# A fused attention and FFN block in f32: transposing y itself, and scaling F by 1/std instead of y

## The chip, the cores and the metric

One core of one Trainium2 chip runs the whole program. The metric is the device time of one execution in microseconds, the median of several runs. TensorE (PE) multiplies matrices and transposes, VectorE (DVE) and ScalarE (ACT) work on its results, GpSimd (POOL) computes small powers, SyncE (SP) issues nearly all DMAs. The engines run on their own and meet only through semaphores.

## The reference

The input x is 8 x 1024 x 256 in f32. What is computed is:

```python
x = x + _layernorm(_L0_attn_ref(_layernorm(x), Wq, Wk, Wv, Wo))   # causal, scaled by 1/16
x = x + _layernorm(_L0_ffn_ref(_layernorm(x), W, b, logits, u))

def _layernorm(x, axis=-1, eps=1e-05):
    m = jnp.mean(x, axis=axis, keepdims=True)
    v = jnp.var(x, axis=axis, keepdims=True)
    return (x - m) / jnp.sqrt(v + eps)

def _L0_ffn_ref(x, W, b, logits, u):
    gumbel = -jnp.log(-jnp.log(u))
    idx = jnp.argmax(jax.nn.log_softmax(logits) + gumbel)
    return jnp.einsum('btd,de->bte', x, W[idx]) + b[idx]
```

The attention has one head of 256 columns; one of eight 256 x 256 FFN matrices is chosen by idx. There are no scales and shifts in the norms.

## The kernel before, in words

The kernel takes the 8 batches one after the other: the first written out, six in a loop on each engine, the last written out with an order of its own. A batch has 1024 rows, 8 tiles of 128; most steps work on a tile or on a pair of tiles.

Each engine runs through a written order of steps, such as PE_ORDER, ACT_ORDER, DVE_ORDER and POOL_ORDER (lines 66 to 73), the PE_LAST and other orders for the last batch, and the PE_BEFORE and other orders for what comes ahead of the first batch. A letter is a kind of step and a number its tile or pair: S scores, M mask and row maximum (DVE), E exponential (ACT), T transposes of the probabilities, V the values, O probabilities times values, R the residual y = x + norm(O) (DVE), N statistics of y, K the normalised yn (ACT), Y the transposes of yn, F the FFN product, U its variance, Z the output, and for the next batch L statistics of x, H its normalising, X its transposes and G the product that the scores need. C is the variance of O.

A product in nearly full precision is made of three f32r passes (`product`, line 800): each operand is split into a rounded half, *_hi, which ACT writes from PSUM, and the rest, *_lo, which DVE writes as PSUM minus *_hi (`subtract_lo`, line 610; its rows have line 613). The lower half's end frees the PSUM bank. Four banks are passed round among the jobs T, V, O, Y, F, X, G in the order in which PE meets them. A job waits (`take_bank`, line 790) until the job four before it has been drained, and until its inputs have been. The scores have four banks of their own (the tensor score), two for even and two for odd tiles.

Around y: R (L741) writes y. N (lines 744 to 757) takes mean and variance of a pair, and writes minus the mean (y_nm) and variance + eps (y_ve). POOL's N step raises y_ve to -0.5 (y_rstd, L387) and makes y_shift = y_nm * y_rstd (L393). ACT's K step (L583) makes yn = y * y_rstd + y_shift, tile by tile. PE's Y step (L932) transposes yn in four pieces, ACT and DVE split it into yT_hi and yT_lo, and PE's F step multiplies with the split weights wf_hi and wf_lo. DVE's F step (L762) adds the bias, one operation for a pair; ACT squares and sums f_sb (L591), DVE's U makes f_ve (L769), POOL f_rstd, and Z (L778) is f_sb * f_rstd + y. For the last batch, Y, F, U, Z have five units, the last two of one tile each, and PE fills gaps with passes on zeros (D, keep_warm).

The FFN matrix and the bias are centred over the output columns ahead of the loop, so that the mean of F is zero: ACT's sums of rows (L470), DVE's neg_mean (L646), ACT's centred (L474). Then ACT makes wf_hi (L502) and DVE wf_lo (L661), both also ahead of the loop, and PE waits for them before the first F. The products of W matrices at L865 are plain f32 matmuls of 256 columns.

## Time and profile before

| | |
|---|---|
| Median of 3 runs | 425.5 us (425.34 to 428.11) |
| Span of the profiled execution | 424.3 us |
| Around the span, against the median | 1.2 us |
| PE busy | 414.0 us, 98% |
| DVE busy | 339.8 us, 80% |
| ACT busy | 299.1 us, 71% |
| POOL busy | 118.3 us, 28% |
| Chain that ended last | PE 93%, DMA 2%, ACT 2%, DVE 1% |
| Granted PE clock | 1.0 in the first slice, 0.9 or more in all others |

The profiled execution has no separate time; its span is what the rows are measured in. A matmul's end is modelled, so the durations of neighbouring matmuls overlap, and distances from start to start are the better measure. On DVE and ACT, too, an operation's start follows its forerunner's start by less than the duration that is shown. Where equal operations follow each other, a timeline merges them to one row with a count (x2).

### The profile page before, as it was taken

What the parts mean: (1) busy time and instruction counts of PE and PEld (TensorE: products, weight loads), DVE (VectorE), ACT (ScalarE), POOL (GpSimd) and SP (SyncE); (2) the same over time, 40 slices, a digit from 0 to 9 for tenths busy, and PEclk for the clock granted to TensorE, in tenths of its full rate; (3) what the DMA queues carried; (4) which work ended last, traced back from release to release, by engine and by line L of the source; (5) the groups of instructions that cost most, each with busy time, mean ns of one, the idle gap of its engine ahead of it and who ended that gap; (6) DMA issues with size and microseconds to landing.
All of it is one profiled execution on the core that took longest, in us unless ns stands there. A gap on an engine that the chain in (4) does not pass through costs nothing.

```text
span 424.3 us, 9812 instructions
## 1 busy us (share of the span) xinstructions
PE 414.0 (98%) x3045; PEld 393.2 (93%) x3045; DVE 339.8 (80%) x1010; ACT 299.1 (71%) x854; POOL 118.3 (28%) x237
## 2 busy tenths in 40 slices
PE   7999999999999999999999999999999999999993
PEld 7789999999999999999999999999999999999993
DVE  4578778987898878887788878898788887876776
ACT  5886877668766687568866687666885678756563
POOL 3103333232322232123421323223232224302133
PEclk9999999999999999999999999999999999999998
DMA  6310012110120101201021001201012000020003
GB/s 198 90 49 26 26 25 76 52 39 14 51 81 18 49 25 42 82 9 40 25 66 57 25 25 48 76 25 49 13 37 99 0 0 0 25 75 2 2 0 101
DMA packets 18951, 18.46 MB, mean 44 GB/s; under 512 B 1140, under 2 KB 18932, under 8 KB 18932
## 3 DMA queue, kind: packets, MB, share of 16 engines
q1 hardware_dynamic: 18660, 17.96, 13.5%
q10 hardware_dynamic: 272, 0.26, 0.2%
q8 instruction: 10, 0.16, 0.2%
q14 instruction: 9, 0.07, 0.1%
HBM read 9.83 MB, written 8.39 MB: 43 GB/s over the span
## 4 chain that ended last, share of the span: by engine, by line
PE 93%; DMA 2%; ACT 2%; DVE 1%; issue 0%; POOL 0%; SPq 0%; POOLq 0%; DVEq 0%
PE bank L805 54%; PE score L805 23%; PE bank L908 7%; PE bank L932 3%; PE bank L819 3%; DMA wq<-in_L_attn_Wq_dram 1%; DMA bias_raw<-in_L_ffn_b_dram 1%; PE score L891 1%; PE score L847 0%; PE bank L865 0%; POOL f_rstd L387 0%; PE score L835 0%; DVE out_sb L778 0%; ACT squares_junk L591 0%; ACT sums_junk L470 0%
## 5 line engine op out<-in xcount | busy, mean ns | idle before, releaser
L387 POOL TENSOR_TENSOR o_rstd<-o_ve,minus_half 128x1 f32<-128x1 f32 x64 | 35.2, 550 | 193.8 <-DVE o_ve L735 193.8
L805 PE MATMUL bank<-v_hi,pT_lo 128*128 128x256 f32 x288 | 84.6, 294 | 0.0
L805 PE MATMUL bank<-v_hi,pT_hi 128*128 128x256 f32 x288 | 81.4, 283 | 0.0
L805 PE MATMUL bank<-v_lo,pT_hi 128*128 128x256 f32 x288 | 81.3, 282 | 0.0
L805 PE MATMUL score<-xT_hi,g_lo 128*128 128x384 f32 (+4 forms) x176 | 63.7, 362 | 0.0
L805 PE MATMUL score<-xT_hi,g_hi 128*128 128x384 f32 (+4 forms) x176 | 61.1, 347 | 0.0
L805 PE MATMUL score<-xT_lo,g_hi 128*128 128x384 f32 (+4 forms) x176 | 61.1, 347 | 0.0
L549 ACT ACTIVATE probs<-neg_scores,neg_max 128x128 f32<-128x128 f32 (+3 forms) x64 | 49.7, 776 | 14.0 <-DVE neg_max L707 13.5
L805 PEld LDWEIGHTS bank<-v_lo,pT_hi 128*128 128x128 f32 x288 | 55.0, 191 | 0.4
L805 PEld LDWEIGHTS bank<-v_hi,pT_lo 128*128 128x128 f32 x288 | 54.9, 191 | 0.3
L805 PEld LDWEIGHTS bank<-v_hi,pT_hi 128*128 128x128 f32 x288 | 54.9, 191 | 0.0
L707 DVE CUSTOM_DVE_ANT_0 neg_scores<-score,mask 128x128 f32<-128x128 f32 (+3 forms) x64 | 48.2, 755 | 7.6 <-PE score L805 7.5
L574 ACT ACTIVATE squares_junk<-bank 128x256 bf16<-128x256 f32 x64 | 24.5, 383 | 40.3 <-PE bank L805 39.8
L613 DVE TENSOR_TENSOR pT_lo<-bank,pT_hi 128x384 fp32r<-128x384 f32 (+2 forms) x96 | 49.6, 551 | 0.8
L441 ACT ACTIVATE pT_hi<-bank 128x384 fp32r<-128x384 f32 (+2 forms) x96 | 43.1, 484 | 2.2 <-PE bank L908 2.0
L908 PE MATMUL bank<-ident,probs 128*128 128x128 f32 x288 | 42.0, 273 | 0.0
L741 DVE SCALAR_TENSOR_TENSOR y<-bank,o_rstd,x_sb 128x256 f32<-128x256 f32 x64 | 30.8, 481 | 11.1 <-POOL o_rstd L387 11.0
L591 ACT ACTIVATE squares_junk<-f_sb 128x256 bf16<-128x256 f32 x64 | 26.3, 419 | 16.7 <-DVE f_sb L762 16.7
L583 ACT ACTIVATE yn<-y,y_shift,y_rstd 128x256 f32<-128x256 f32 x64 | 35.0, 597 | 4.3 <-POOL y_shift L393 4.3
L387 POOL TENSOR_TENSOR f_rstd<-f_ve,minus_half 128x2 f32<-128x2 f32 (+1 forms) x33 | 24.1, 731 | 49.6 <-DVE f_ve L769 49.6
L805 PE MATMUL bank<-wf_hi,yT_lo 128*128 128x256 f32 x128 | 37.3, 292 | 0.4 <-DVE yT_lo L613 0.4
L805 PE MATMUL bank<-wvo_hi,xT_lo 128*128 128x256 f32 x128 | 36.9, 288 | 0.0
(112 smaller groups left out, 1130.5 us busy)
## 6 DMA issues: line engine op xcount, KB each, us to landing
x_sb<-in_L_attn_x_dram SPq DMA_DIRECT2D x32, 256.0 KB, 2.7
out_dram<-out_sb SPq DMA_DIRECT2D x31, 256.0 KB, 2.1
wq<-in_L_attn_Wq_dram ACTq DMA_DIRECT2D x1, 256.0 KB, 4.1
wk<-in_L_attn_Wk_dram SPq DMA_DIRECT2D x1, 256.0 KB, 4.4
wv<-in_L_attn_Wv_dram SPq DMA_DIRECT2D x1, 256.0 KB, 4.2
wo_raw<-in_L_attn_Wo_dram SPq DMA_DIRECT2D x1, 256.0 KB, 4.5
wf_raw<-in_L_ffn_W_dram SPq DMA_DIRECT2D x1, 256.0 KB, 2.7
out_dram<-out_sb SPq DMA_DIRECT2D x2, 128.0 KB, 2.1
```

Source lines behind the costliest of these rows:

```text
L387: return nc.gpsimd.tensor_tensor(dst[:, n0:n1], ve[:, n0:n1], minus_half[:, n0:n1], ALU.pow)
L441: nc.scalar.activation(dst, src, ACT.Identity).then_inc(hi_ready, 1)
L549: nc.scalar.activation(probs[:, n % 2, here], neg_scores[:, n % 2, here], ACT.Exp, scale=-1.0, bias=neg_max[:, n:n + 1], accum_out=exp_sum ...
L574: nc.scalar.activation(squares_junk[:, 0, n, :], cols(job.bank, D), ACT.Square, accum_out=o_ss[:, n:n + 1])
L583: last = nc.scalar.activation(yn[:, p, t % 2, :], y[:, t, :], ACT.Identity, bias=y_shift[:, t:t + 1], scale=y_rstd[:, t:t + 1])
L591: last = nc.scalar.activation(squares_junk[:, 1, t, :], f_sb[:, p, t % 2, :], ACT.Square, accum_out=f_ss[:, t:t + 1])
L613: nc.vector.tensor_tensor(dst, src, hi.bitcast(f32), ALU.subtract).then_inc(bank_drained[job.bank], 1)
L707: nc.vector.tensor_tensor_reduce(out=masked.rearrange("p (h w) -> p h w", h=h), in0=score[:, n % 2, 0:h, 0:w], in1=mask[:, here].rearrange ...
L741: nc.vector.scalar_tensor_tensor(out=y[:, n, :], in0=cols(job.bank, D), scalar=o_rstd[:, n:n + 1], in1=x_tile(b, n), op0=ALU.mult, op1=ALU ...
L805: last = nc.tensor.matmul(dst, l, r, start=(i == 0), stop=(i == len(passes) - 1))
L819: last = nc.tensor.transpose(cols(job.bank)[:, (2 * k + t) * PART:(2 * k + t + 1) * PART], xn[:, 2 * p + t, k * PART:(k + 1) * PART], iden ...
L908: last = nc.tensor.transpose(cols(job.bank)[:, (t - t0) * PART:(t - t0 + 1) * PART], probs[:, n % 2, t * PART:(t + 1) * PART], ident[:, :])
```

## The change

The mean of y is no longer taken away before the FFN. Instead the FFN matrix, already centred over its columns, is centred over its rows of input too, so that a constant in y contributes nothing. PE computes the means itself: two f32 products of a 128 x 128 matrix that is full of 1/256 with the two halves of wf, into score's bank for odd tiles, before S2 of the first batch. DVE subtracts them from wf after M2 of the first batch. ACT's wf_hi follows E3 and DVE's wf_lo follows M5 of the first batch; both have left the orders ahead of the loop.

PE's Y step transposes y, and waits for the drained O jobs of its tiles instead of for yn. ACT's K steps are gone, and so are y_nm, y_shift and yn. POOL's N step makes y_rstd alone. DVE's F step waits for y_rstd as well, and is one operation for each tile: bank * y_rstd + bias, 128 x 256.

The diff, without the declarations of buffers and semaphores:

```diff
@@ -65,8 +65,8 @@
 
     PE_ORDER = """S0 V0 S1 V1 T0 S2 T1 S3 O0 V2 T2 O1 S4 T3 V3 O2 S5 O3 T4 S6 T5 S7 X0 Y0 O4 T6 O5 T7 O6 X1 Y1
         O7 F0 G0 Y2 X2 F1 X3 F2 Y3 G1 G2 F3 G3"""
-    ACT_ORDER = """V0 E0 E1 V1 T0 E2 O0 T1 V2 T2 O1 E3 H0 T3 V3 E4 O2 O3 E5 T4 K0 T5 E6 K1 X0 Y0 O4 T6 E7 O5 T7
-        H1 H2 O6 Y1 H3 X1 O7 K2 G0 Y2 F0 X2 K3 X3 F1 Y3 F2 G1 G2 F3 G3"""
+    ACT_ORDER = """V0 E0 E1 V1 T0 E2 O0 T1 V2 T2 O1 E3 H0 T3 V3 E4 O2 O3 E5 T4 T5 E6 X0 Y0 O4 T6 E7 O5 T7
+        H1 H2 O6 Y1 H3 X1 O7 G0 Y2 F0 X2 X3 F1 Y3 F2 G1 G2 F3 G3"""
     DVE_ORDER = """M0 M1 L0 V0 M2 T0 V1 L1 T1 C0 M3 R0 V2 L2 T2 M4 C1 V3 T3 R1 N0 M5 C2 C3 R2 R3 N1 M6 T4 T5 M7
         X0 Y0 C4 R4 T6 C5 L3 R5 T7 C6 N2 R6 X1 Y1 C7 F0 R7 N3 G0 Y2 F1 U0 X2 Z0 X3 F2 U1 Y3 U2 Z1 G1
         F3 Z2 U3 G2 G3 Z3"""
@@ -75,8 +75,8 @@
 
     PE_LAST = """V0 S0 V1 S1 T0 S2 V2 T1 S3 O0 T2 O1 S4 T3 S5 O2 T4 O3 S6 V3 T5 O4 S7 Y0 T6 O5 T7 O6 Y1 F0 O7
         Y2 F1 F2 Y3 D11 Y4 F3 D12 F4"""
-    ACT_LAST = """E0 V0 V1 T0 E1 V2 T1 E2 O0 E3 T2 O1 T3 E4 T4 O2 O3 E5 K0 E6 V3 T5 O4 Y0 T6 E7 O5 K1 T7 O6 Y1
-        K2 F0 O7 Y2 K3 Y3 F1 K4 Y4 F2 F3 F4"""
+    ACT_LAST = """E0 V0 V1 T0 E1 V2 T1 E2 O0 E3 T2 O1 T3 E4 T4 O2 O3 E5 E6 V3 T5 O4 Y0 T6 E7 O5 T7 O6 Y1
+        F0 O7 Y2 Y3 F1 Y4 F2 F3 F4"""
     DVE_LAST = """M0 V0 M1 M2 V1 T0 V2 T1 C0 M3 M4 C1 R0 T2 R1 T3 N0 M5 C2 R2 C3 T4 M6 R3 V3 N1 C4 T5 R4 M7 Y0
         T6 C5 R5 T7 N2 C6 F0 R6 Y1 U0 N3 C7 Y2 F1 R7 N4 F2 Y3 U1 Z0 Z1 Y4 U2 F3 U3 F4 Z2 U4 Z3 Z4"""
     POOL_LAST = """C0 C1 C2 N0 C3 N1 C4 C5 N2 C6 U0 N3 C7 N4 U1 U2 U3 U4"""
@@ -85,8 +85,8 @@
 
 
     PE_BEFORE = "D22 W0 W1 D13 X0 A0 X1 D25 W2 G0 D6 X2 X3 G1 A1 G2 G3"
-    ACT_BEFORE = "W0 H0 J0 H1 X0 A0 X1 B0 H2 H3 G0 J1 X2 X3 G1 U0 A1 U1 G2 U2 G3 E0"
-    DVE_BEFORE = "L0 L1 W1 B0 J0 L2 L3 X0 A0 X1 W2 B1 G0 X2 X3 U0 G1 A1 U1 G2 G3"
+    ACT_BEFORE = "W0 H0 J0 H1 X0 A0 X1 B0 H2 H3 G0 J1 X2 X3 G1 U0 A1 U1 G2 G3 E0"
+    DVE_BEFORE = "L0 L1 W1 B0 J0 L2 L3 X0 A0 X1 W2 B1 G0 X2 X3 U0 G1 A1 G2 G3"
 
     def steps_of(text):
         return [(w[0], int(w[1:])) for w in text.split()]
...
@@ -377,6 +376,7 @@
             pool.wait_ge(memsets, 1)
             nc.gpsimd.affine_select(out=ident[:, :], in_=ident[:, :], compare_op=ALU.not_equal, fill=1.0, base=0,
                                     pattern=[[-1, PART]], channel_multiplier=1).then_inc(consts_ready, 1)
+            nc.gpsimd.memset(averaging[:, :], 1.0 / D)
             nc.gpsimd.memset(mask[:, :], 0.0).then_inc(memsets, 1)
             pool.wait_ge(memsets, 2)
 
@@ -410,7 +410,7 @@
                     elif kind == "N":
 
                         pool.wait_ge(y_ve_ready, b * NP + n + 1)
-                        scales(y_nm, y_ve, y_rstd, y_shift, t0, t1).then_inc(y_shift_ready, 1)
+                        rstd(y_rstd, y_ve, t0, t1).then_inc(y_rstd_ready, 1)
                     elif kind == "U":
 
                         pool.wait_ge(f_ve_ready, b * NP + n + 1)
@@ -498,7 +498,7 @@
                         centred(2 + m, wf_raw[:, m, :], wf[:, m, :])
                     centred(4, bias_raw[:, :], bias[:, :]).then_inc(wf_centred, 1)
                 else:
-                    act.wait_ge(wf_centred, 1)
+                    act.wait_ge(wf_twice_centred, 1)
                     nc.scalar.activation(wf_hi[:, :, :], wf[:, :, :], ACT.Identity).then_inc(wf_hi_ready, 1)
 
             for kind, n in steps_of(ACT_BEFORE):
@@ -534,7 +534,7 @@
                     nc.scalar.activation((wvo_hi if n else a_hi)[:, :, :],
                                          cols(job.bank).rearrange("p (m n) -> p m n", m=KC), ACT.Identity, scale=1.0 if n else -SCALE).then_inc(hi_ready, 1)
 
-            def sequence(b, last_one=False):
+            def sequence(b, last_one=False, first=False):
                 def at(kind, n, g=0):
                     return Job(b, last_one, kind, n, g)
 
@@ -549,6 +549,8 @@
                         nc.scalar.activation(probs[:, n % 2, here], neg_scores[:, n % 2, here], ACT.Exp, scale=-1.0,
                                              bias=neg_max[:, n:n + 1],
                                              accum_out=exp_sums[:, n:n + 1]).then_inc(probs_ready, 1)
+                        if first and n == 3:
+                            ffn_weights(2)
                     elif kind == "T":
                         for g, (t0, t1) in enumerate(t_groups(n)):
                             job = at("T", n, g)
@@ -576,13 +578,6 @@
 
                         nc.scalar.activation(o_ez[:, n:n + 1], exp_sums[:, n:n + 1], ACT.Square,
                                              scale=EPS ** 0.5).then_inc(o_squares, 1)
-                    elif kind == "K":
-
-                        act.wait_ge(y_shift_ready, b * NP + n + 1)
-                        for t in range(t0, t1):
-                            last = nc.scalar.activation(yn[:, p, t % 2, :], y[:, t, :], ACT.Identity,
-                                                        bias=y_shift[:, t:t + 1], scale=y_rstd[:, t:t + 1])
-                        last.then_inc(yn_ready, 1)
                     elif kind == "F":
                         job = at("F", n)
 
@@ -592,7 +587,7 @@
                                                         accum_out=f_ss[:, t:t + 1])
                         last.then_inc(f_squares, 1)
 
-            sequence(0)
+            sequence(0, first=True)
             with act.Fori(1, B - 1) as b:
                 sequence(b)
             sequence(B - 1, True)
@@ -655,11 +650,6 @@
                     negative_means(0, 2, 1)
                 elif kind == "U" and n == 0:
                     negative_means(2, 5, 2)
-                elif kind == "U":
-
-                    dve.wait_ge(wf_hi_ready, 1)
-                    nc.vector.tensor_tensor(wf_lo[:, :, :], wf[:, :, :], wf_hi[:, :, :].bitcast(f32),
-                                            ALU.subtract).then_inc(wf_ready, 1)
                 elif kind == "B" and n == 0:
                     dve.wait_ge(choice_loaded, 32)
                     nc.vector.tensor_reduce(lse[:, 0:1], logits[:, :], AX.X, ALU.max, negate=True).then_inc(choice_dve, 1)
@@ -688,7 +678,7 @@
 
             dve.wait_ge(mask_ready, 1)
 
-            def sequence(b, last_one=False):
+            def sequence(b, last_one=False, first=False):
                 def at(kind, n, g=0):
                     return Job(b, last_one, kind, n, g)
 
@@ -709,6 +699,17 @@
                                                        in1=mask[:, here].rearrange("p (h w) -> p h w", h=h),
                                                        scale=1.0, scalar=3e38, op0=ALU.add, op1=ALU.min,
                                                        accum_out=neg_max[:, n:n + 1]).then_inc(max_ready, 1)
+                        if first and n == 2:
+
+                            dve.wait_ge(wf_means_ready, 1)
+                            nc.vector.tensor_tensor(wf[:, :, :], wf[:, :, :],
+                                                    score[:, 1:2, 1, 0:D].broadcast_to([PART, KC, D]),
+                                                    ALU.subtract).then_inc(wf_twice_centred, 1)
+                        elif first and n == 5:
+
+                            dve.wait_ge(wf_hi_ready, 1)
+                            nc.vector.tensor_tensor(wf_lo[:, :, :], wf[:, :, :], wf_hi[:, :, :].bitcast(f32),
+                                                    ALU.subtract).then_inc(wf_ready, 1)
                     elif kind == "T":
                         for g, (t0, t1) in enumerate(t_groups(n)):
                             job, here = at("T", n, g), slice(t0 * PART, t1 * PART)
@@ -752,17 +753,19 @@
                             last = nc.vector.bn_aggr(y_mv[:, t, :], y_stats[:, t, :])
                         last.then_inc(y_mv_ready, 1)
                         dve.wait_ge(y_mv_ready, b * NP + n + 1)
-                        nc.vector.tensor_scalar(y_nm[:, t0:t1], y_mv[:, t0:t1, 0], -1.0, None, ALU.mult)
                         nc.vector.tensor_scalar(y_ve[:, t0:t1], y_mv[:, t0:t1, 1], EPS, None,
                                                 ALU.add).then_inc(y_ve_ready, 1)
                     elif kind == "F":
                         job = at("F", n)
 
                         dve.wait_ge(bank_full[job.bank], job.used + 1)
-                        nc.vector.tensor_tensor(f_sb[:, p, here, :],
-                                                cols(job.bank, (t1 - t0) * D).rearrange("p (t d) -> p t d", t=t1 - t0),
-                                                bias[:, None, :].broadcast_to([PART, t1 - t0, D]),
-                                                ALU.add).then_inc(bank_drained[job.bank], 1)
+                        dve.wait_ge(y_rstd_ready, b * NP + n + 1)
+                        for t in range(t0, t1):
+                            last = nc.vector.scalar_tensor_tensor(out=f_sb[:, p, t % 2, :],
+                                                                  in0=bank[job.bank][:, (t - t0) * D:(t - t0 + 1) * D],
+                                                                  scalar=y_rstd[:, t:t + 1], in1=bias[:, :],
+                                                                  op0=ALU.mult, op1=ALU.add)
+                        last.then_inc(bank_drained[job.bank], 1)
                     elif kind == "U":
 
                         dve.wait_ge(f_squares, b * NP + n + 1)
...
@@ -884,6 +887,15 @@
 
                             g = g_job(b, 2 * (n // (NT // 2)) + 1)
                             pe.wait_ge(bank_drained[g.bank], g.used + 1)
+                        if first and n == 2:
+
+                            pe.wait_ge(wf_centred, 1)
+                            for k in range(KC):
+                                means = nc.tensor.matmul(score[:, 1, 1, 0:D], averaging[:, :], wf[:, k, :], start=(k == 0),
+                                                         stop=(k == KC - 1))
+                            means.then_inc(wf_means_ready, 1)
+                        elif first and n == 5:
+                            pe.wait_ge(wf_twice_centred, 1)
                         h, w = pieces(n)
                         if w < 2 * PART:
 
@@ -925,12 +937,11 @@
                                 ).then_inc(bank_full[job.bank], 1)
                     elif kind == "Y":
 
-                        pe.wait_ge(yn_ready, b * NP + n + 1)
                         job = at("Y", n)
-                        take_bank(job)
+                        take_bank(job, *(at("O", t) for t in range(t0, t1)))
                         for i, (k, t) in enumerate((k, t) for k in range(KC) for t in range(t0, t1)):
                             last = nc.tensor.transpose(cols(job.bank)[:, i * PART:(i + 1) * PART],
-                                                       yn[:, p, t % 2, k * PART:(k + 1) * PART], ident[:, :])
+                                                       y[:, t, k * PART:(k + 1) * PART], ident[:, :])
                         last.then_inc(bank_full[job.bank], 1)
                     elif kind == "F":
                         if first and n == 0:
```

## Rows read from the trace of the kernel before

**Rows 1.** page, part 1: busy us, share of the span, instructions of each engine.
```profile
PE 414.0 (98%) x3045; PEld 393.2 (93%) x3045; DVE 339.8 (80%) x1010; ACT 299.1 (71%) x854; POOL 118.3 (28%) x237
```

**Rows 2.** waits of TensorE: engine, what, releaser: us in total, times, longest.
```profile
PE score L835 <- POOL ident L378: 1.7, 1, 1.7
PE bank L932 <- ACT yn L583: 1.1, 1, 1.1
PE score L847 <- DMA wq<-in_L_attn_Wq_dram: 0.7, 1, 0.7
PE score L891 <- DVE wvo_lo L682: 0.6, 1, 0.6
PE bank L805 <- DVE xT_lo L613: 0.4, 1, 0.4
PE bank L805 <- DVE yT_lo L613: 0.4, 2, 0.3
```

**Rows 3.** groups by line and shape: busy us, mean ns, idle before, releaser.
```profile
L583 ACT ACTIVATE yn<-y,y_shift,y_rstd 128x256 f32<-128x256 f32 x64 | 35.0, 597 | 4.3 <-POOL y_shift L393 4.3
...
L741 DVE SCALAR_TENSOR_TENSOR y<-bank,o_rstd,x_sb 128x256 f32<-128x256 f32 x64 | 30.8, 481 | 11.1 <-POOL o_rstd L387 11.0
L778 DVE SCALAR_TENSOR_TENSOR out_sb<-f_sb,f_rstd,y 128x256 f32<-128x256 f32 x64 | 28.1, 480 | 2.7 <-POOL f_rstd L387 2.7
...
L762 DVE TENSOR_TENSOR f_sb<-bank,bias 128x512 f32<-128x512 f32 x31 | 21.4, 689 | 7.6 <-PE bank L805 7.6
...
L755 DVE TENSOR_SCALAR y_nm<-y_mv 128x2 f32<-128x2 f32 x31 | 5.3, 170 | 1.1
...
L707 DVE CUSTOM_DVE_ANT_0 neg_scores<-score,mask 128x384 f32<-128x384 f32 x8 | 4.5, 558 | 2.3 <-PE score L805 2.3
...
L865 PE MATMUL bank<-wo,wT 128*128 128x256 f32 x8 | 1.9, 379 | 0.0
...
L762 DVE TENSOR_TENSOR f_sb<-bank,bias 128x256 f32<-128x256 f32 x2 | 0.8, 422 | 0.0
```

**Rows 4.** VectorE in order of time, third batch: start us, us, what, idle before.
```profile
165.57 0.69 DVE L762 TENSOR_TENSOR f_sb<-bank,bias 128x512 f32<-128x512 f32 x1 [0.16 <-PE bank L805]
166.18 0.16 DVE L769 TENSOR_SCALAR f_ve<-f_ss 128x2 f32<-128x2 f32 x1
166.25 0.68 DVE L613 TENSOR_TENSOR xT_lo<-bank,xT_hi 128x512 fp32r<-128x512 f32 x1
167.21 0.88 DVE L778 SCALAR_TENSOR_TENSOR out_sb<-f_sb,f_rstd,y 128x256 f32<-128x256 f32 x2 [0.28 <-POOL f_rstd L387]
168.01 0.69 DVE L613 TENSOR_TENSOR xT_lo<-bank,xT_hi 128x512 fp32r<-128x512 f32 x1
```

**Rows 5.** TensorE in order of time, same batch: the transposes of Y3.
```profile
167.23 0.60 PE L932 MATMUL bank<-ident,yn 128*128 128x128 f32 x4
```

**Rows 6.** VectorE in order of time, first batch: v_lo of pair 1.
```profile
29.73 0.68 DVE L613 TENSOR_TENSOR v_lo<-bank,v_hi 128x512 fp32r<-128x512 f32 x1
```

**Rows 7.** TensorE in order of time, first batch: first matmul of V2.
```profile
30.70 0.28 PE L805 MATMUL bank<-wvo_hi,xT_lo 128*128 128x256 f32 x1
```

**Rows 8.** TensorE in order of time, the end: Y4 and F4.
```profile
416.09 0.44 PE L932 MATMUL bank<-ident,yn 128*128 128x128 f32 x2 [1.14 <-ACT yn L583]
...
418.18 0.36 PE L805 MATMUL bank<-wf_hi,yT_lo 128*128 128x256 f32 x1 [0.25 <-DVE yT_lo L613]
```

**Rows 9.** VectorE in order of time, the end: out_sb of pair 1, yT_lo of Y4.
```profile
416.81 0.88 DVE L778 SCALAR_TENSOR_TENSOR out_sb<-f_sb,f_rstd,y 128x256 f32<-128x256 f32 x2 [0.27 <-POOL f_rstd L387]
417.61 0.42 DVE L613 TENSOR_TENSOR yT_lo<-bank,yT_hi 128x256 fp32r<-128x256 f32 x1
```

**Rows 10.** busy us of PE, PEld, DVE, ACT, POOL by stretch; clock, DMA share, GB/s.
```profile
415.00:420.00 5.00, 2.78 (x26) 2.39 (x26) 3.88 (x13) 3.11 (x14) 2.33 (x5) 1.00 0.27 86
420.00:425.00 5.00, 0.00 (x0) 0.00 (x0) 1.31 (x4) 0.13 (x2) 0.72 (x1) 0.69 0.38 128
```

More of the change, by code:

```diff
@@ L188, in sandwich_block_kernel @@
         y = sb("y", [PART, NT, D])
-        yn = sb("yn", [PART, NP, 2, D])
         yT_hi = sb("yT_hi", [PART, NP, KC, 2, PART], f32r)
@@ L210, in sandwich_block_kernel @@
         y_ve = sb("y_ve", [PART, NT])
-        y_nm = sb("y_nm", [PART, NT])
-        y_shift = sb("y_shift", [PART, NT])
         y_rstd = sb("y_rstd", [PART, NT])
@@ L238, in sandwich_block_kernel @@
         ident = sb("ident", [PART, PART])
+        averaging = sb("averaging", [PART, PART])
         mask = sb("mask", [PART, S])
@@ L267, in sandwich_block_kernel @@
         y_ve_ready = sem("y_ve_ready")
-        y_shift_ready = sem("y_shift_ready")
-        yn_ready = sem("yn_ready")
+        y_rstd_ready = sem("y_rstd_ready")
         f_squares = sem("f_squares")
@@ L297, in sandwich_block_kernel @@
         wf_centred = sem("wf_centred")
+        wf_means_ready = sem("wf_means_ready")
+        wf_twice_centred = sem("wf_twice_centred")
         wf_hi_ready = sem("wf_hi_ready")
@@ L781, in sequence @@
                         last.then_inc(out_ready, 1)
-            sequence(0)
+            sequence(0, first=True)
             with dve.Fori(1, B - 1) as b:
```

## The prediction

> **What bounds the kernel now.** I read the busy times first. TensorE is busy 414.0 of 424.3 us, VectorE 339.8, ScalarE 299.1 [rows 1]; the reader is to see that only 10.3 us of the span are left in which TensorE does nothing at all. The view of waits comes second: TensorE waits 1.7 + 1.1 + 0.7 + 0.6 + 0.4 + 0.4 = 4.9 us in the whole run, six entries, none of which is met once per batch [rows 2]. So in the batches TensorE never stands still, and the work that the change takes away (ScalarE's normalising of y, VectorE's negated mean) isn't on the path. What can move the time is (a) work added to TensorE, (b) waits that arise because VectorE hands something over later than today, and (c) the two ends of the run. The profiled execution has a span of 424.3 us; the median of the three runs is 425.5, 1.2 above it. I work against the span and add 1.2.
>
> **Removed.** ScalarE loses the 64 yn operations, 35.0 us [rows 3]. Their cover: TensorE waited for yn once, 1.1 us [rows 2], so for the batches this is worth nothing. VectorE loses y_nm, 31 operations; between two short ones it takes some 0.08 us of the queue, so about 0.3 us per batch. GpSimd loses the y_shift product and its drain; nobody waits on GpSimd for it but ScalarE's yn. PE's Y step has the same four transposes, and waits for y instead of yn; y exists earlier than yn, always. It keeps its place in TensorE's order, so nothing behind it moves.
>
> **Added in each batch: F.** Today F is one addition of 128x512 at 689 ns; afterwards it is two 128x256 multiply-and-adds, of the kind of L741 (481 ns, PSUM and SBUF in) or L778 (480) [rows 3]. Counted from start to start, today's F takes 166.18 - 165.57 = 0.61 us of the queue, and a pair of L778 takes 168.01 - 167.21 = 0.80 [rows 4]. Each F thus makes VectorE 0.20 us later, four times a batch, 0.8 us, against 0.3 given back. VectorE has idle time for that on average (85 us over the run), but what counts is the place. Behind F of the second pair stand f_ve and then xT_lo of pair 2, at 166.25, which ends at 166.93 [rows 4]. That step frees the bank that TensorE's Y3 takes at 167.23 [rows 5]: a margin of 0.30 us. What is the least distance from a VectorE end to TensorE's start? The last F of the run did wait: yT_lo ended at 417.61 + 0.42 = 418.03 and TensorE began at 418.18 [rows 8, 9], 0.15 us. Later by 0.20, the margin is 0.10 and TensorE stands still for 0.05 us. (F1 itself is paced by TensorE, [rows 4] show it idle for 0.16 before, so lateness from F0 isn't added.) Seven batches have this order: **+0.35 us**. F also waits for a second semaphore, y_rstd, which is long there; if the second wait instruction costs some 0.05 us behind the first, the stall is 0.1 per batch, +0.7 in all. Its lower bound is nothing, if the margin is a little larger than I read; the upper bound is that all four F's lateness arrives, below. I take 0.35, since the two rows give it directly.
>
> On whether such an F is dear, the row comes first: L778 has two f32 tensors from SBUF and takes 480 ns, L741 with one of them in PSUM takes 481 [rows 3]. The Trainium skill, page "Vector Engine (DVE) Microarchitecture Reference", list of pitfalls at its end, says that a scalar_tensor_tensor with two SBUF sources that are not bf16 runs at half throughput. By that, L778 would have to be dearer than L741 by another pass over 256 elements, and it isn't; F would then cost 0.53 us more, and the batches would be VectorE's. The trace disagrees, and I go by the row.
>
> **Added once: second centring of the FFN weights.** (1) TensorE gets two f32 (not f32r) products of 256 columns ahead of S2 of the first batch. Of that kind is L865: four calls make 8 instructions, 1.9 us busy [rows 3], so two calls make 4 instructions, 0.95 us by that, and TensorE has no free time there: **+0.9**. Bounds: 0.75, since the modelled ends overlap (379 ns is the mean of one, but 8 fill 1.9 us), and 1.0 with the change from one kind of matmul to the other. (2) VectorE subtracts the means, 128x512 like today's F, 0.6 us of its queue, between M2 and T0. M2 is a step before which VectorE waits for TensorE (2.3 us in eight, [rows 3]), so earlier VectorE time doesn't cover it. Behind it, v_lo of pair 1 at 29.73, ends 30.41 [rows 6], and frees the bank of TensorE's V2, which begins at 30.70 [rows 7]: margin 0.28. Later by 0.60 the wait is 0.60 - 0.28 + 0.15 = **+0.47**. Steps behind it are late by the same 0.6, but TensorE is by then 0.47 later itself. Bounds: 0, if the work that left the preamble makes up for it, and 0.6, the whole subtraction. (3) wf_hi and wf_lo move from ahead of the loop into the first batch, behind E3 and M5. wf_lo's 0.6 us lands where VectorE waits for ScalarE and GpSimd soon after; wf_hi's operation lands on a ScalarE that loses 2.2 us of yn soon after. Ahead of the loop VectorE no longer waits for wf_hi, but TensorE's wait there is for wvo_lo (0.6, [rows 2]), made before. Nothing either way. The memset of the averaging matrix is short and stands behind ident.
>
> **The end.** TensorE's 1.1 us wait for yn is before Y4, at 416.09 [rows 8]. Without it Y4 goes right after the filler. But its yT_lo stands in VectorE's queue behind the two out_sb of pair 1, which start at 416.81 and wait for a square sum and GpSimd, not for yn; yT_lo starts at 417.61 as they end [rows 9]. That chain begins with ScalarE's squares of F1, which follow Y3. So what is late next is f_rstd, and the 1.1 us come back as TensorE idling later. The single-tile F3 and F4 are in that chain and go from 422 to 481 ns each [rows 3]: **+0.1**.
>
> **Sum:** 0.9 + 0.47 + 0.35 + 0.1 = +1.8, with a share of the second wait +1.9: span 426.2, time 427.4 us, 0.4% above the median.
>
> **Rivals.**
> A, VectorE in the way (slower). Lateness of F isn't absorbed at TensorE's places, since all four F steps, two-wait overhead included (0.26 each), less 0.3, reach the T1 of the next batch: 0.72 us a batch, 5.0 in seven, 424.3 + 5.0 + 1.4 + 0.1 + 1.2 = 432.0. It decides once VectorE has no idle between F3 and M2 of the next batch. Against it: that idle before M2, 2.3/8 = 0.29 us each [rows 3]. For it: only 0.15 to 0.3 us of margin at several places.
> B, nothing stalls. VectorE and ScalarE start the first batch earlier since the wf work left the preamble, and F's 0.2 us is absorbed: only 0.9 of TensorE work, time 426.4.
> C, the wait for yn did set the end. Y4, F3 and their squares come 1.1 us earlier: 427.4 - 1.1 = 426.3. For it, the wait is real; against it, the place of yT_lo in VectorE's queue.
> D, faster: ScalarE's 35 us make TensorE run closer. Even if all 4.9 us of its waits [rows 2] went, 425.5 - 4.9 + 0.9 = 421.5. The start's 1.7 and 0.7 are for ident and Wq, which the change doesn't touch.
> E, the clock at the end. The granted clock is 1.00 in 415 to 420, with TensorE busy for 2.78 of 5 us, and 0.69 on average in the next 5, where it does nothing [rows 10], so it does fall to the 1.2 GHz level after a rest. With Y4 and F3 moved up, TensorE rests longer ahead of F4; if the clock fell there, F4's 0.7 us double: 428.1. The Trainium skill, "TensorE: Matmul & The Clock Gate", Part 1, says that the engine is slowed by rest and freed by activity; the trace agrees in this row, but the rest ahead of F4 would stay under 1.2 us.
>
> **How the numbers follow.** Forecast 0.51; B 0.20; C 0.13; A 0.08; D 0.03; E 0.03; the rest is unnamed. B and C lie within 1.1 us below the forecast, and both together would give 425.3, so the range begins at 425.4; it ends at 429.3, where not quite half of A's lateness arrives. About 1% (4.3 us) is what a measurement of this kernel can tell from no change. Slower by more needs A almost in full or more than one mishap: 0.08. Faster by more needs D: 0.03. Within: 0.89.
>
> **What would show it.** Right: TensorE busy rises by about 0.9 us, with 4 new instructions around 28 us; ScalarE falls by some 35 us; f_sb rows of 480 ns x64; a new TensorE wait for v_lo of about 0.3 to 0.5 us once; a wait for xT_lo of 0.05 us in each batch, so a period of TensorE from batch to batch that is up by under 0.1. The yn wait is gone, and before F4 TensorE waits over 1 us for yT_lo. Wrong: a period up by 0.5 us or more (A), an unchanged period and no v_lo wait (B), or a last out_sb that comes 1 us earlier after F0 (C).

## The result, and the profile after

| | before | after |
|---|---|---|
| Median of the compared runs | 426.08 us (425.34 to 428.11, 14 runs) | 428.69 us (427.86 to 432.43, 14 runs) |
| Ratio after to before | | 1.0065, interval 1.0051 to 1.0080 |
| Span of the profiled execution | 424.3 us | 426.5 us |

The change makes the kernel 2.6 us slower, 0.65%, which is within the 1% that the prediction counts as no change, and inside its range. Forecast were 427.4 us in time and 426.2 in span.

The page after, busy times:

```profile
PE 416.5 (98%) x3049; PEld 394.7 (93%) x3049; DVE 343.6 (81%) x1009; ACT 268.2 (63%) x790; POOL 112.0 (26%) x205
```

ScalarE is busy 30.9 us less than in [rows 1], where some 35 was forecast, and none of it reached the time. TensorE has four instructions more and is busy for 2.5 us more. The forecast gave it 0.9, so most of the difference isn't new work. Its waits, in the columns of [rows 2]:

```profile
PE score L838 <- POOL ident L377: 1.7, 1, 1.7
PE bank L808 <- DVE yT_lo L608: 1.4, 2, 0.7
PE bank L808 <- DVE xT_lo L608: 0.7, 1, 0.7
PE score L850 <- DMA wq<-in_L_attn_Wq_dram: 0.6, 1, 0.6
PE score L903 <- DVE wvo_lo L672: 0.2, 1, 0.2
```

The sum is 4.6 us, 0.3 less than before. The wait for yn is gone, and the wait for yT_lo has gone from 0.4 to 1.4 in its place. F's group on VectorE has another form, and the averaging is a new one on TensorE (columns as in [rows 3]):

```profile
L764 DVE SCALAR_TENSOR_TENSOR f_sb<-bank,y_rstd,bias 128x256 f32<-128x256 f32 x64 | 28.0, 478 | 5.6 <-PE bank L808 5.2
...
L894 PE MATMUL score<-wf,averaging 128*128 128x256 f32 x4 | 1.0, 380 | 0.0
```

**Where the time went.** TensorE shows no rest in the loop, so its own marks divide the run: S0, the first scores of each batch. Its rows in the timeline of TensorE (start us, us) of the first, second and last batch, before:

```profile
23.34 0.71 PE L891 MATMUL score<-xT_first,g_first 128*128 128x128 f32 x4 [0.64 <-DVE wvo_lo L682]
...
73.45 0.61 PE L891 MATMUL score<-xT_first,g_first 128*128 128x128 f32 x4
...
374.36 0.61 PE L891 MATMUL score<-xT_first,g_first 128*128 128x128 f32 x4
```

and after:

```profile
22.49 0.71 PE L903 MATMUL score<-xT_first,g_first 128*128 128x128 f32 x4 [0.20 <-DVE wvo_lo L672]
...
73.94 0.60 PE L903 MATMUL score<-xT_first,g_first 128*128 128x128 f32 x4
...
376.31 0.61 PE L903 MATMUL score<-xT_first,g_first 128*128 128x128 f32 x4
```

| us | start of S0 | first batch | six batches | last part | span |
|---|---|---|---|---|---|
| before | 23.34 | 50.11 | 300.91 | 49.9 | 424.3 |
| after | 22.49 | 51.45 | 302.37 | 50.2 | 426.5 |
| difference | -0.85 | +1.34 | +1.46 | +0.3 | +2.2 |

The first batch costs 1.34 us, nearly all of it the averaging and the subtraction, as forecast. The six batches cost 0.24 us each, where the forecast had 0.05, and they have no new wait in the view of waits, which doesn't list the shortest ones. The start is no firm gain: over all seven traces of versions of the kernel before, S0 starts between 22.61 and 24.34 us (mean 23.5), over the seven of the kernel after between 22.49 and 23.26 (mean 22.9).

What makes six batches longer in which TensorE shows as busy all the time? Counting starts of its instructions in 124 to 174 us (columns as in [rows 10]), before and after:

```profile
124.00:174.00 50.00, 50.00 (x369) 47.73 (x369) 41.93 (x126) 36.08 (x104) 14.40 (x28) 1.00 0.14 42
```

```profile
124.00:174.00 50.00, 50.00 (x367) 47.67 (x366) 42.17 (x125) 32.05 (x96) 13.60 (x24) 1.00 0.13 41
```

At the same granted clock of 1.00 it starts two matmuls less in 50 us. Worked out from all rows of the timeline, the 256-column products of V stand 119.6 ns apart from start to start after and 116.9 before, those of F 119.7 and 117.7 (means within a step). A batch has 48 of each: 48 x 2.7 + 48 x 2.0 = 0.23 us. The work is the same, at a closer or wider spacing. This isn't the whole account: the 24 products of 512 columns of G stand about 2 ns closer after, which gives back 0.05 us, and a short stall of 0.09 us at F3 is new (below, under F on VectorE).

### The profile page after: what moved, and what is told of

Its sections match the earlier page's. It is cut to its first block, busy times and chain, and to the rows that moved or that the text cites. A ratio compares the mean times of both kernels' runs of the same rounds, so it can differ in the third digit from the quotient of the medians.

```text
span 426.5 us, 9687 instructions
## 1 busy us (share of the span) xinstructions
PE 416.5 (98%) x3049; PEld 394.7 (93%) x3049; DVE 343.6 (81%) x1009; ACT 268.2 (63%) x790; POOL 112.0 (26%) x205
## 4 chain that ended last, share of the span: by engine, by line
PE 92%; DVE 3%; issue 1%; ACT 1%; POOL 1%; DMA 1%; POOLq 0%; SPq 0%; DVEq 0%
PE bank L808 54%; PE score L808 23%; PE bank L920 7%; PE bank L943 3%; PE bank L822 3%; PE score L903 1%; DMA bias_raw<-in_L_ffn_b_dram 1%; DVE f_sb L764 1%; ACT sums_junk L470 0%; POOL f_rstd L387 0%; DVE xT_lo L608 0%; DVE out_sb L781 0%; ACT xn L464 0%; DVE x_stats L622 0%; POOL mask L380 0%
## 5 line engine op out<-in xcount | busy, mean ns | idle before, releaser
L808 PE MATMUL bank<-wf_hi,yT_hi 128*128 128x256 f32 x128 | 36.2, 283 | 0.0
```

The costliest lines, as they stand in the source:

```text
L808: last = nc.tensor.matmul(dst, l, r, start=(i == 0), stop=(i == len(passes) - 1))
```

## The experiments

Each ratio is to the kernel before, run beside the variant, and its interval follows in brackets.

The theory going in was that the first batch is slower by the new work, and the loop by where the buffers lie: the change takes out yn (8192 bytes of each partition), y_nm and y_shift (32 bytes each) and adds averaging (512), and everything declared behind them moves. Summed from the declarations, a, wvo and wf lie at 64 modulo 128 bytes before and at 0 after. The rivals: VectorE's longer F makes many short waits that the view doesn't list, or the batches differ by chance from one version or run to another.

**after_pad64**: 64 unused bytes put back ahead of the weights.

```diff
+        pad64 = sb("pad64", [PART, 16])
         wq = sb("wq", [PART, KC, D])
```

> The changed kernel with an unused buffer of 64 bytes a partition ahead of wq, so that wvo and wf again begin at 64 modulo 128 bytes, as they did in the kernel before; nothing else differs. The trace of the changed kernel has V and F matmuls of 256 columns 120 ns apart where they were 117 to 118 apart before, and a batch period of 50.15 us against 49.92. Theory A (address): the moving operand's place modulo 128 bytes sets the distance; V and F come back to 117 to 118 ns, the batch period to 49.95 to 50.00, the time falls by 1.0 to 1.4 us. Theory B (VectorE in the way, as predicted): the pad changes nothing; period 50.15, same time.

Measured: 428.71 us (426.96 to 431.06), ratio 1.0055 (1.0019 to 1.0090), span 425.8. S0 in its trace:

```profile
74.64 0.61 PE L904 MATMUL score<-xT_first,g_first 128*128 128x128 f32 x4
...
375.84 0.61 PE L904 MATMUL score<-xT_first,g_first 128*128 128x128 f32 x4
```

Six batches take 301.20 us instead of 302.37, the last part 0.2 less, the first 0.07 less: 1.4 us between S0 and the end come from nothing but the place of buffers. V's spacing is 117.2 ns and F's 117.3. The median of the times does not show this by itself, since its interval is as wide as the effect; the traces do, and before_again and after_again (below) say how far they can be trusted.

**before_pad64**: the same 64 bytes in the kernel before, the same edit.

> The kernel before with the same unused 64 bytes ahead of wq, which moves wvo and wf to 0 modulo 128 bytes, the place they have in the changed kernel. Theory A (address): V and F matmuls go from 117-118 to 120 ns apart, the batch period from 49.92 to 50.10, plus 1.2 to 1.5 us, though no instruction differs. Theory B (VectorE in the way): no change, period 49.92.

Measured: 427.20 us (425.94 to 428.10), ratio 1.0012 (0.9989 to 1.0035), span 424.3. First batch 50.23, six batches 301.42: 0.5 us more than before in six batches, not 1.2. V and F went to 119.0 and 118.8 ns, but the 512-column products of G from 233.4 to 232.4, faster. So the places of a, wvo and wf modulo 128 matter, but aren't the whole rule: the theory wanted 1.2 to 1.5 us.

**before_fpairs**: F as two additions of 128x256, without a scale.

```diff
-                        nc.vector.tensor_tensor(f_sb[:, p, here, :],
-                                                cols(job.bank, (t1 - t0) * D).rearrange("p (t d) -> p t d", t=t1 - t0),
-                                                bias[:, None, :].broadcast_to([PART, t1 - t0, D]),
-                                                ALU.add).then_inc(bank_drained[job.bank], 1)
+                        for t in range(t0, t1):
+                            last = nc.vector.tensor_tensor(f_sb[:, p, t % 2, :],
+                                                           bank[job.bank][:, (t - t0) * D:(t - t0 + 1) * D],
+                                                           bias[:, :], ALU.add)
+                        last.then_inc(bank_drained[job.bank], 1)
```

> The kernel before with F's addition of the bias made in two operations of 128x256 instead of one of 128x512; no scaling, no second wait. It isolates VectorE's lateness. Theory B as the prediction had it: each F takes 0.80 instead of 0.60 us of VectorE's queue, TensorE waits 0.05 us for xT_lo before Y3 in each batch, period 49.97, plus 0.3 to 0.5 us. Theory A gives no more than that here. If lateness of all four F reached TensorE, the period would be 50.6 and the time 5 us more.

Measured: 426.80 us, ratio 1.0004 (0.9980 to 1.0027), span 425.3, of which 1.0 is a later first S0 (24.31); first batch 50.12, six batches 300.91, the same as before.

**before_stt**: F as two multiply-and-adds with a constant in the place of y_rstd.

```diff
+                            last = nc.vector.scalar_tensor_tensor(out=f_sb[:, p, t % 2, :],
+                                                                  in0=bank[job.bank][:, (t - t0) * D:(t - t0 + 1) * D],
+                                                                  scalar=1.0, in1=bias[:, :],
+                                                                  op0=ALU.mult, op1=ALU.add)
```

> The kernel before with F made in two scalar_tensor_tensor of 128x256 (bank * 1.0 + bias), without the wait for y_rstd. before_fpairs used two additions, which took only 0.07 us more of the queue (margin ahead of Y3 0.23 instead of 0.30) and stopped nothing. Theory B (VectorE's lateness by 0.20 us per F): here the margin is 0.10, TensorE waits before Y3, the period goes from 49.92 to 49.96, +0.3 us in all, and if the changed kernel's remaining 0.045 us per batch (with 64 bytes of padding) came from the second wait, this one stays at 49.92.

Measured: 426.07 us, ratio 0.9989 (0.9964 to 1.0013), span 423.9, six batches 300.81. The groups of F in the two, before_fpairs first:

```profile
L763 DVE TENSOR_TENSOR f_sb<-bank,bias 128x256 f32<-128x256 f32 x64 | 24.1, 417 | 6.3 <-PE bank L806 4.9
```

```profile
L763 DVE SCALAR_TENSOR_TENSOR f_sb<-bank,bias 128x256 f32<-128x256 f32 x64 | 24.2, 419 | 6.2 <-PE bank L807 4.9
```

The multiplication costs nothing, 419 ns to 417. The change's F has 478: the 60 ns come with the scale read from memory, one value for each partition. And a pair in VectorE's order of time, before_stt and then after:

```profile
165.21 0.76 DVE L763 SCALAR_TENSOR_TENSOR f_sb<-bank,bias 128x256 f32<-128x256 f32 x2
165.89 0.16 DVE L771 TENSOR_SCALAR f_ve<-f_ss 128x2 f32<-128x2 f32 x1
```

```profile
166.47 0.88 DVE L764 SCALAR_TENSOR_TENSOR f_sb<-bank,y_rstd,bias 128x256 f32<-128x256 f32 x2
167.26 0.16 DVE L772 TENSOR_SCALAR f_ve<-f_ss 128x2 f32<-128x2 f32 x1
167.33 0.68 DVE L608 TENSOR_TENSOR xT_lo<-bank,xT_hi 128x512 fp32r<-128x512 f32 x1
```

0.68 us of the queue against 0.79, and 0.61 for the one addition of before [rows 4]: of the 0.18 us by which F is longer, 0.07 come from two operations in the place of one, and 0.11 from the scale. So neither before_fpairs nor before_stt makes VectorE as late as the change does, and that their batches are no longer doesn't show that the change's F is free.

**after_nomeans**: after_pad64 without the averaging products, without the subtraction, and with wf_hi waiting for the first centring only. It leaves the second centring out.

> The changed kernel with the 64 bytes of padding, and without the second centring: neither the two products with the averaging matrix nor the subtraction of the means are made, so the output lacks the removal of y's mean. Expected by the prediction's terms: the first batch from V0 to V0 of the next takes 51.27 with them and 50.05 without; of the 1.2 to 1.3 us 0.7 is TensorE's work and the rest waits at O0 and V2. If the first batch stays above 50.5, something else in it (wf_hi, wf_lo moved) costs.

Measured: 426.00 us, ratio 0.9994 (0.9974 to 1.0015), span 424.0.

```profile
22.91 0.71 PE L889 MATMUL score<-xT_first,g_first 128*128 128x128 f32 x4 [0.74 <-DVE wvo_lo L673]
...
72.95 0.61 PE L889 MATMUL score<-xT_first,g_first 128*128 128x128 f32 x4
```

First batch 50.04 us: all of the first batch's cost, 51.38 - 50.04 = 1.34 us, is the second centring, and wf_hi and wf_lo, which moved into this batch, cost nothing. The six batches take 301.10, 0.03 us each above before.

**after_late**: after_pad64, with VectorE's subtraction behind M3 instead of M2.

```diff
-                        if first and n == 2:
+                        if first and n == 3:
```

> The changed kernel with the 64 bytes of padding, and VectorE's subtraction of the means after M3 instead of M2; TensorE's products stay. If the waits at O0 and V2 of the first batch come from the 0.6 us between M2 and T0, they go away, and the first batch falls from 51.27 to 50.85 to 50.95, with 0.7 to 0.9 us of TensorE's own work left. If they came from TensorE's products alone, nothing changes.

Measured: 427.07 us, ratio 1.0024 (1.0003 to 1.0044), span 425.6.

First batch 50.90 us (S0 at 23.26 and 74.16), 0.48 less than after_pad64 with the same work. So the place of the subtraction costs 0.48 of the 1.34, and 0.86 is left for the averaging. The six batches take 301.42 us. Their loop and the places of their buffers are those of after_pad64 (301.20) and after_nomeans (301.10): three such kernels differ by up to 0.05 us per batch, so a difference of that size between two versions isn't firm.

**after_tail**: the kernel after, with one step of VectorE's order for the last batch moved.

```diff
-        ... F2 Y3 U1 Z0 Z1 Y4 U2 F3 U3 F4 Z2 U4 Z3 Z4
+        ... F2 Y3 U1 Z0 Y4 U2 F3 Z1 U3 F4 Z2 U4 Z3 Z4
```

> The changed kernel with VectorE's order at the end of the last batch changed: yT_lo of Y4, U2 and F3 ahead of the out_sb pair of Z1. The prediction said that the removed wait for yn gives nothing, since Y4's yT_lo stands behind Z1, which waits for f_rstd. If so, the 1 us shows here: F4 on TensorE starts about 1.1 us earlier relative to F0 of the last batch, the end comes 0.8 to 1.1 us earlier, time minus 1.0. If the chain of U1 and Z1 set the end by itself, nothing changes.

Measured: 427.79 us, ratio 1.0042 (1.0019 to 1.0065), span 425.7; from the last S0 to the end 49.3 us instead of 50.2. VectorE's yT_lo of Y4 no longer stands behind out_sb of pair 1, and F4 on TensorE has no wait; the one before F3 stays. The two rows, VectorE's and TensorE's:

```profile
418.73 0.42 DVE L608 TENSOR_TENSOR yT_lo<-bank,yT_hi 128x256 fp32r<-128x256 f32 x1
...
419.54 0.36 PE L808 MATMUL bank<-wf_hi,yT_lo 128*128 128x256 f32 x1
```

**before_place**: the kernel before, with four paddings of 64 bytes, ahead of v_hi, neg_scores, wq and wo_raw. Modulo 128 bytes v goes from 0 to 64, and a, with the W matrices declared ahead of it, from 64 to 0, and the rest stays.

```diff
+        pad_v = sb("pad_v", [PART, 16])
         v_hi = sb("v_hi", [PART, NT, D], f32r)
         v_lo = sb("v_lo", [PART, NT, D], f32r)
+        pad_s = sb("pad_s", [PART, 16])
         neg_scores = sb("neg_scores", [PART, 2, S])
...
+        pad_w = sb("pad_w", [PART, 16])
         wq = sb("wq", [PART, KC, D])
...
+        pad_o = sb("pad_o", [PART, 16])
         wo_raw = sb("wo_raw", [PART, KC, D])
```

> The kernel before with four unused buffers of 64 bytes: v_hi and v_lo begin at 64 modulo 128 bytes (before: 0), a_hi and a_lo at 0 (before: 64), wvo and wf stay at 64. No instruction differs. Theory A (address of the moving operand): O's matmuls, 108 of 256 columns in a batch, go from 120 to 117-118 ns, G's with the stationary operand at 0 from 234 to 231; the batch period falls from 49.92 to about 49.6 and the time by 2 to 2.5 us. If only the distance of wvo and wf to other buffers matters and not their place modulo 128, nothing changes.

Measured: 422.52 us (422.08 to 423.24), ratio 0.9905 (0.9874 to 0.9936), span 421.3, first batch 49.74, six batches 298.37. It does the same work as before, instruction by instruction.

In 124 to 174 us it starts 373 matmuls, four more than before, at the same granted clock of 1.00.

**before_v64**: only the two paddings around v.

> The kernel before with two unused buffers of 64 bytes, so that v_hi and v_lo alone begin at 64 modulo 128 bytes. (neg_scores and all behind it are 128 bytes further.) Theory A (address of the moving operand): only O changes, from 119.5 to 116.5-117 ns, 108 matmuls a batch, so the period goes from 49.92 to 49.6; G and S stay at 233 and 232. If G and S come down here too, as they did in before_place (229 and 227), what counts isn't each matmul's own operand alone.

Measured: 421.80 us (420.57 to 424.07), ratio 0.9899 (0.9855 to 0.9943), span 420.8; six batches 297.34, 3.6 less than before and 1.0 less than before_place. So the paddings around v are what gains, and the two others beside them gain nothing. The step is the product O; a product that reads v_lo and the third such product behind it:

```profile
139.63 0.28 PE L807 MATMUL bank<-v_lo,pT_hi 128*128 128x256 f32 x1
...
140.66 0.28 PE L807 MATMUL bank<-v_lo,pT_hi 128*128 128x256 f32 x1
```

Between the two stand nine distances, 1.03 us here and 1.07 at the same place of before_again (139.94 to 141.01), 114 and 119 ns each. But V (115.1 instead of 116.9), F (116.9 instead of 117.7) and the 512-column G (230.8 instead of 233.4) went faster too, and their own operands lie where they lay modulo 128; modulo 256 all that is declared behind v has moved. A rule that looks at one matmul's moving operand alone, modulo 128, falls by this.

**before_again and after_again**: both kernels as they are, once more.

> The kernel before, unchanged, as a control for the readings by which the theories are told apart: the distances between matmuls and the batch period. If they belong to the kernel and not to the run or the chip, the period is 49.92 us again and the mean distance of V 117, of F 118, of O 119.5 ns, with a ratio of 1.000 and an interval that takes in 1. If the distances wander from run to run by 2 ns, the address theory has nothing to stand on.

> The changed kernel, unchanged, as the second control. Period 50.15 us, V and F 119.6 ns apart again, if the distances belong to the kernel; time 2.6 to 2.8 us above before.

Measured: 426.14 us (ratio 0.9996, 0.9972 to 1.0020) and 428.89 (1.0092, 1.0059 to 1.0124). The six batches take 300.91 and 302.25, against 300.91 and 302.37 in the first traces: they agree within 0.02 us per batch. The spacing belongs to the kernel, not to the execution.

**after_best**: the kernel after, with v at 64, a at 0, wvo and wf back at 64, the subtraction behind M3 and the tail of after_tail.

```diff
+        pad_v = sb("pad_v", [PART, 16])
...
+        pad_s = sb("pad_s", [PART, 16])
...
+        pad_o = sb("pad_o", [PART, 16])
...
-                        if first and n == 2:
+                        if first and n == 3:
```

> The changed kernel with all that the runs point to: v, wvo and wf at 64 modulo 128 bytes and a at 0, the subtraction of the means after M3, and yT_lo of Y4, U2 and F3 ahead of Z1 at the end. From the single steps: 0.24 to 0.42 + 0.2 us a batch for the places (4 to 5 us), 0.5 for the subtraction, 0.75 for the end. Time 422.5 to 424, ratio 0.992 to 0.996: faster than before, and still slower than the kernel before with the same places (0.9905), since TensorE's 0.7 us of averaging and F's 0.07 us a batch are left.

Measured: 422.08 us (421.59 to 423.56), ratio 0.9906 (0.9877 to 0.9935), span 420.2; first batch 50.38, six batches 297.94, last part 48.9. It is as fast as before_place, and 6.6 us under the kernel after. Most of that is places, (302.37 - 297.94) = 4.4 us in the six batches alone. It came out 0.4 us under the range that was expected, and it doesn't beat the kernel before with its own best places: before_v64 has 421.80 us and 297.34 in six batches, 0.10 less per batch.

## Why the prediction was right and where it was not

**Averaging on TensorE, +0.9: right.** The last transpose ahead of it, the four new instructions, and the first two matmuls of S2 after:

```profile
26.62 0.27 PE L920 MATMUL bank<-ident,probs 128*128 128x128 f32 x1
26.73 1.03 PE L894 MATMUL score<-wf,averaging 128*128 128x256 f32 x4
27.41 0.52 PE L808 MATMUL score<-xT_hi,g_lo 128*128 128x384 f32 x1
27.77 0.34 PE L808 MATMUL score<-xT_lo,g_hi 128*128 128x384 f32 x1
```

The same transpose and the second matmul of S2 in after_nomeans:

```profile
27.01 0.27 PE L906 MATMUL bank<-ident,probs 128*128 128x128 f32 x1
...
27.30 0.33 PE L803 MATMUL score<-xT_lo,g_hi 128*128 128x384 f32 x1
```

From the transpose to that matmul it is 1.15 us with the averaging and 0.29 without: 0.86 us, of which the instructions themselves take 0.68 (27.41 - 26.73) and the changes between kinds of matmul the rest. after_late leaves 0.86 as well, by the batches.

**Subtraction on VectorE, +0.47: right size, but the wait is in two places.** after_late gives 0.48. The forecast had one wait, before V2; most of it is before O0. TensorE in the first batch after:

```profile
30.03 0.40 PE L808 MATMUL score<-xT_hi,g_hi 128*128 128x512 f32 x1
30.47 0.35 PE L808 MATMUL bank<-v_hi,pT_lo 128*128 128x256 f32 x1
30.66 0.28 PE L808 MATMUL bank<-v_lo,pT_hi 128*128 128x256 f32 x1
30.78 0.28 PE L808 MATMUL bank<-v_hi,pT_hi 128*128 128x256 f32 x1
30.98 0.39 PE L808 MATMUL bank<-wvo_hi,xT_lo 128*128 128x256 f32 x1
31.20 0.28 PE L808 MATMUL bank<-wvo_lo,xT_hi 128*128 128x256 f32 x1
```

and VectorE:

```profile
29.44 0.68 DVE L705 TENSOR_TENSOR wf<-wf,score 128x512 f32<-128x512 f32 x1
30.04 0.28 DVE L608 TENSOR_TENSOR pT_lo<-bank,pT_hi 128x128 fp32r<-128x128 f32 x1
30.24 0.68 DVE L608 TENSOR_TENSOR v_lo<-bank,v_hi 128x512 fp32r<-128x512 f32 x1
```

O0 comes 0.44 us after its forerunner's start instead of 0.23, since pT_lo ends at 30.32, 0.15 earlier, and its second matmul 0.19 later instead of 0.11. V2 comes 0.20 after its forerunner instead of 0.12; its record is 0.11 longer than its like, and the second matmul follows 0.22 later instead of 0.12. v_lo ends at 30.92, so 0.15 behind it would be 31.07, which falls into that longer record. That is 0.21 + 0.08 at O0 and 0.08 + 0.10 at V2, 0.47 of the 0.48. The view of waits lists none of them: short waits show only as distances. The prediction passed over pT_lo, which stands ahead of v_lo in VectorE's queue.

**F on VectorE, +0.05 per batch: right in size, wrong in place.** The forecast had TensorE wait for xT_lo before Y3. TensorE after, the last product of F2 and Y3:

```profile
168.02 0.28 PE L808 MATMUL bank<-wf_hi,yT_hi 128*128 128x256 f32 x1
168.15 0.60 PE L943 MATMUL bank<-ident,y 128*128 128x128 f32 x4
```

xT_lo ends at 167.33 + 0.68 = 168.01, and the distance of 0.30 in [rows 4, 5] has shrunk to 0.14, as the prediction said. But Y3 starts 0.12 us behind the last product of F2, just as it does before: it doesn't stall. The stall is at F3, which waits for VectorE's yT_lo of Y3. VectorE's yT_lo and TensorE's first two matmuls of F3, before and after:

```profile
169.27 0.69 DVE L613 TENSOR_TENSOR yT_lo<-bank,yT_hi 128x512 fp32r<-128x512 f32 x1
170.47 0.28 PE L805 MATMUL bank<-wf_hi,yT_lo 128*128 128x256 f32 x1
170.59 0.28 PE L805 MATMUL bank<-wf_lo,yT_hi 128*128 128x256 f32 x1
```

```profile
170.54 0.68 DVE L608 TENSOR_TENSOR yT_lo<-bank,yT_hi 128x512 fp32r<-128x512 f32 x1
171.37 0.35 PE L808 MATMUL bank<-wf_hi,yT_lo 128*128 128x256 f32 x1
171.56 0.28 PE L808 MATMUL bank<-wf_lo,yT_hi 128*128 128x256 f32 x1
```

From the end of yT_lo to F3 it was 0.51 us before, and it is 0.15 after, in each of the six batches of the loop. F1 and F2 both stand ahead of yT_lo in VectorE's queue, and their lateness adds up: 2 x 0.18 = 0.36. before_stt and before_fpairs bear this out, with 0.37 left, 2 x 0.07 less than before. The prediction followed only one F's lateness to the next step. After, the second matmul of F3 comes 0.19 us behind the first instead of 0.12, and the first some 0.02 later than it did: about 0.09 us per batch, in after as in after_pad64. Of this the period shows 0.05 in after_pad64, 0.03 in after_nomeans and 0.09 in after_late, the differences being within what such versions differ by.

The second wait, for y_rstd, costs nothing on the path: the pair takes 0.79 us of the queue, the 0.80 that the prediction took from L778. On the price of such an F: the Trainium skill, "Vector Engine (DVE) Microarchitecture Reference", section "Points that are easy to get wrong", has half the throughput for this operation with two sources from SBUF that are not bf16. The traces don't agree: out_sb, which has two in f32, takes 479 ns, and f_sb, which has one, 478. F's own two tensors are one in PSUM and one in SBUF, so the 0.53 us that the prediction worked out for it by that page had no ground even there. What is dear, by the runs, is the scale from memory, 478 ns to 419.

**The end, +0.1: right, and rival C falls.** By after_pad64 the last part is 0.06 us longer. Y4 no longer waits, and F3 and F4 wait for their yT_lo in its place, the one of F4 behind out_sb in VectorE's queue, as the prediction had it:

```profile
417.36 0.41 DVE L608 TENSOR_TENSOR yT_lo<-bank,yT_hi 128x256 fp32r<-128x256 f32 x1
...
418.91 0.88 DVE L781 SCALAR_TENSOR_TENSOR out_sb<-f_sb,f_rstd,y 128x256 f32<-128x256 f32 x2 [0.27 <-POOL f_rstd L387]
419.71 0.42 DVE L608 TENSOR_TENSOR yT_lo<-bank,yT_hi 128x256 fp32r<-128x256 f32 x1
```

```profile
417.92 0.36 PE L808 MATMUL bank<-wf_hi,yT_lo 128*128 128x256 f32 x1 [0.67 <-DVE yT_lo L608]
...
420.27 0.36 PE L808 MATMUL bank<-wf_hi,yT_lo 128*128 128x256 f32 x1 [0.72 <-DVE yT_lo L608]
```

Before F4 it is 0.72 us, not over 1 as the prediction wanted, because 0.67 come already before F3. Before, F3 (at 416.29) had no wait and F4 one of 0.25 [rows 8], so what has come is 0.67 + 0.47 = 1.14: just what the wait for yn was. after_tail shows that 0.9 us of gain was there to be had, hidden by the order alone. In the kernel before, the same order could have given TensorE at most the 0.25 us that F4 waited; no run tries it.

**The other rivals.** A wanted 0.72 us per batch and the batches have 0.24, of which VectorE has about 0.09; its mechanism, lateness that adds up over several F steps, is there, but only F1 and F2 count, and the margin that F3 had takes up nearly all of their 0.36 us. B wanted an unchanged period and no wait in the first batch. D wanted waits of TensorE to go: their sum fell by 0.3 us. E wanted a lower clock at F4. The granted clock is 1.00 in 415 to 420 us, and in the stretch with F4 (columns as in [rows 10]):

```profile
420.00:425.00 5.00, 0.94 (x6) 0.77 (x6) 2.89 (x10) 1.02 (x4) 1.97 (x3) 0.94 0.50 167
```

F4 starts at 420.27 and its matmuls stay 0.12 us apart: that is the 2.4 GHz level. The clock is 1.00 in 420 to 421.3, where F4 is TensorE's last work, and in 421.3 to 424 too; only 424 to 426.5 has 0.57. (In the kernel before, the last slice of the page has 0.8, not 0.9 or more as the table of its profile says; the fall, in 421 to 422, lies behind TensorE's last work there too.)

**What failed: the list of parts.** "It keeps its place in TensorE's order, so nothing behind it moves" is true of instructions and not of addresses. Taking out yn moved every buffer behind it, and the prediction gave that no term at all. By after_pad64 it is 0.07 + 1.17 + 0.18 = 1.4 us. The rest is 1.27 in the first batch, 0.29 in the six and 0.06 in the last part, 1.6, where the forecast had 1.8 to 1.9. Together that is the 3.0 measured from the first S0 on, 404.0 - 401.0 (span less start of S0). That the forecast of the span, 426.2, came within 0.3 of the trace is luck: an earlier start of 0.85 hid most of the missing term.

The median came 1.3 us above the forecast, 428.7 against 427.4, for two reasons. The kernel before has 426.08 over 14 runs, not the 425.5 of its first three, so the step from span to time isn't 1.2 us: the profiled execution after took 428.29 with a span of 426.5, 1.8 more, and so do nearly all others. That is 0.6. The other 0.7 is the change itself, 2.6 us instead of 1.9.

**Open:** by what rule the place of buffers sets the spacing of matmuls. Shown is that it does, that v's place moves it most, that it repeats from run to run, and that the place of one operand modulo 128 bytes doesn't predict it. Whether it is modulo 256, a meeting of two operands, or of TensorE's reads with those of other engines, no run here tells apart. Open too is how much of the earlier start (0.85 us in this trace, 0.6 in the mean of seven against seven) comes from the weights' work that left the stretch ahead of the loop.

## What to carry to other kernels

Where TensorE is never idle, a buffer added or taken away can change the time as much as the edit itself, by the places of all that is declared behind it; pad it back before a small difference is put down to the edit, and try a few paddings of 64 bytes for their own sake. Measure such a kernel by the distance between the same mark in successive batches: in two traces of the same kernel it repeats to 0.02 us, where a median's interval is 1 us and more to either side; between two versions, even with the same loop and places, take 0.05 us for noise. A wait taken away at the end of a run pays only when the next engine's order lets the following step through. And when an engine gets slower in several steps, follow the sum of its lateness to every step that waits for it, not to the nearest one alone.

## What the runs showed of the hardware

- The distance of 256-column f32r matmuls from start to start goes from 115 to 120 ns with the places of buffers, at a granted clock of 1.00. For the whole kernel that is 1%, 421.8 us (before_v64) against 426.
- A multiply-and-add of 128x256 on VectorE takes 419 ns with a constant, 478 with one value for each partition; an addition takes 417.
- TensorE starts 0.14 to 0.15 us after the end of the VectorE operation that it waits for (F3 in the loop, O0 in the first batch, F3 and F4 at the end), and after such a stop the second matmul is late as well, 0.19 us behind the first instead of 0.12.
- Two calls of a plain f32 product of 256 columns are four instructions and cost TensorE 0.86 us with the changes from and to f32r.
